# A Swin block on one core: FC2 in float16 with its scale in PSUM, tokens turned in spans of 112, and the step loop written out

## The chip, the core and the metric

The kernel runs on one core of a Trainium2 chip. A core has TensorE (PE; its weight loads are shown apart as PEld), VectorE (DVE), ScalarE (ACT), GpSimd (POOL) and SyncE (SP, which here issues all DMAs). Each has its own instruction stream, and they wait for each other through semaphores. Products are written to PSUM, which the kernel uses as eight banks of 512 float32 columns; GpSimd works on SBUF alone here. The metric is the device time of one execution in microseconds, the median of several runs.

## The reference

A window-attention block on x of 32 x 96 x 56 x 56 (float32): layer norm over the 96 channels, a shift by 3, windows of 7 x 7 = 49 tokens, 12 heads of 8 channels, a mask for the shifted borders, a projection, then an MLP of 96 -> 192 -> 96 with an exact GELU, and two residuals.

```python
f = _ln(x.transpose(0, 2, 3, 1), g1, b1); f = jnp.roll(f, (-SS, -SS), axis=(1, 2))
qkv = _window_partition(f) @ w_qkv + b_qkv                      # -> q, k, v
attn = softmax(q @ k.T * scale + mask); out = (attn @ v) @ w_proj + b_proj
f = residual + roll(_window_reverse(out), (SS, SS))
m = _ln(f, g2, b2)
m = jax.nn.gelu(m @ w_fc1 + b_fc1, approximate=False) @ w_fc2 + b_fc2
return f + m
```

## The kernel before, in words

**Tiling.** The image is cut into bands of seven rows: eight windows, 392 tokens (`TOK`). There are 32 x 8 = 256 bands. A tile has channels on partitions and a band's 392 tokens in the free dimension, or tokens on partitions. All products that need precision are made of float16 halves: weights and tokens are split into a high and a low part, and three products (high x high, high x low, low x high) are summed in PSUM, with the weights times `GAIN` = 64.

**Pipeline.** Work is a pipeline over steps. In step t each engine runs a fixed list of stages, each for another band: `LOAD` for band t+9, `TURN` for t+6, `BACK` for t+5, `QK` for t+4, `VALUES` and `SCORE` for t+2, `PROB` for t, `WEIGH` for t-1, and in pairs `HIDDEN` (FC1 and GELU), `RESULT` (FC2) and `STORE` for bands around t-5 to t-7. Odd and even steps have different lists: FC1 and GELU of two bands stand in the odd step (`expand`, `expand_rest`, `gelu`), FC2 of two bands at the end of PE's even step (`contract`). The order in each engine is written by hand; each engine takes its instructions strictly in that order. What a stage must wait for is counted from the band's number.

**The loop.** `steps` (L186) writes out the steps -9 to 8, then a `Fori` loop of seven rounds of 32 steps, then the rest. In the loop the counts that semaphores are compared with are computed from a register.

**The token turns (L516, L541).** PE's `turn` transposes the normalised-to-be tokens from channels on partitions to tokens on partitions: x of band t+6 (tile `xw`) and, for the second layer norm, the residual sum of eight bands earlier (tile `f`). Each is four transposes of 98 tokens into one bank each (D and D+1). ACT (even steps) or DVE (odd steps) copies them to `tok`; DVE makes statistics per group of 98 tokens (`bn_stats`, `bn_aggr`, eight groups); POOL's `normalise` makes `xn` (subtract the mean, a power of -1/2, multiply); PE's `back` transposes the eight groups back into banks B and B+1, ACT's `back_high` (L703) writes the float16 high part `xfh`, DVE's `back_low` (L844) the low part `xfl`.

**FC2 (L620).** `contract` waits for `gelu_done` and the free banks D, D+1, and multiplies in float32, which the trace records as two passes per product:

```python
for s in range(2):
    dst = psum[0:C, D + n, s * PART:(s + 1) * PART]
    nc.tensor.matmul(dst, w2[:, 0, :], hid[:, b.c % 2, s, :], start=True, stop=False)
    last = nc.tensor.matmul(dst, w2[:, 1 + s, :], hid[:, b.c % 2, 2, :], start=False, stop=True)
```

POOL's `add_bias` (L370) adds the FC2 bias to `f` beforehand, and DVE's `result` (L864) adds `f` and the bank into `yr`, which SP stores.

**What stands around FC2.** In the even step PE's list ends with `out_transposes` (L591), `back` (L553), `max_transpose` (L580), `queries_keys` (L420), `project` (L601), `contract` 0 and 1 (L632, L633). The odd step's list begins with `shifted(t, 0)` (L494), which waits for `stack_in`, `max_in` and, at L489, for `n_low` of the even step's `back`; then `values` (L455) and `scores(t, 0)` (L476), which waits for `qk_low`. ACT in the even step: `queries_keys_high` (nat, L714), then `back_high` (xfh, L706), then the odd step's `exps` (L694). DVE: `back_low` (L847), `queries_keys_low` (L854), `result`. POOL in each step: `normalise`, `order_x` (copies a loaded band into window order), `add_bias`.

## Time and profile before

| | |
|---|---|
| median of 3 runs | 2933.02 us (2930.35 to 2939.53) |
| the profiled execution | 2936.45 us, its span 2934.7 us |
| mean granted TensorE clock | 0.994 |
| PE busy | 2835.0 us, 97% of the span |
| DVE busy | 2404.5 us, 82% |
| ACT busy | 2000.5 us, 68% |
| POOL busy | 1758.0 us, 60% |
| DMA | 359.65 MB, mean 123 GB/s |

Busy is the union of an engine's instruction times. Matmuls overlap each other, so the distance from one start to the next tells what one costs in a stream, not its own length. The chain is followed back from the last instruction: at each step to whatever ended the wait, so its shares tell which engine's work made up the span. "Issue" is time in the chain in which the profile shows nothing that was waited for.

### The profile page before, as it was taken

How to read it: one execution, taken by the hardware profiler on the slowest of the kernel's cores; microseconds unless marked ns; L12 is line 12 of the kernel's file. 1: busy time of each engine (PE TensorE's matmuls, PEld its weight loads, DVE VectorE, ACT ScalarE, POOL GpSimd, SP SyncE). 2: the span in 40 equal slices, each digit the busy share in tenths (PEclk: the TensorE clock that was granted, in tenths of full speed). 3: DMA queues.
4: the chain of work that ended last, by engine and by line, in shares of the span. 5: the costliest groups of instructions: out<-in, count | busy, mean ns of one | idle time of the engine just before them, and what ended most of it. 6: DMA issues, size and time to landing. Idle time of an engine off the chain costs nothing.

```text
span 2934.7 us, 141485 instructions
## 1 busy us (share of the span) xinstructions
PE 2835.0 (97%) x54820; PEld 2387.2 (81%) x54820; DVE 2404.5 (82%) x7142; ACT 2000.5 (68%) x3208; POOL 1758.0 (60%) x2088
## 2 busy tenths in 40 slices
PE   4999999999999999999999999999999999999997
PEld 2788888888878888888888888878888788888886
DVE  6888887888878888788888888878888788888885
ACT  2676776777767777667766776767777677677674
POOL 3566566566656666565665666656666556656655
PEclk9999999999999999999999999999999999999999
DMA  3444454445444554444444444445445444444441
GB/s 83 121 130 127 127 130 120 129 122 131 130 118 120 129 131 121 123 126 130 122 131 122 128 128 130 124 118 130 130 119 133 117 129 128 127 126 129 125 117 43
DMA packets 414934, 359.65 MB, mean 123 GB/s; under 512 B 63646, under 2 KB 414176, under 8 KB 414204
## 3 DMA queue, kind: packets, MB, share of 16 engines
q1 hardware_dynamic: 414220, 350.04, 45.8%
q8 instruction: 459, 7.52, 1.1%
q14 instruction: 255, 2.09, 0.2%
HBM read 193.29 MB, written 154.14 MB: 118 GB/s over the span
## 4 chain that ended last, share of the span: by engine, by line
PE 90%; ACT 5%; issue 2%; DVE 2%; POOL 0%; SPq 0%; DMA 0%; DVEq 0%; ACTq 0%; POOLq 0%
PE psum L512 19%; PE psum L494 11%; PE psum L420 8%; PE psum L476 8%; PE psum L538 7%; PE psum L553 6%; PE psum L601 6%; PE psum L632 6%; PE psum L633 6%; PE psum L430 5%; ACT probs L694 4%; PE psum L591 3%; PE psum L438 3%; PE psum L455 2%; PE psum L580 1%
## 5 line engine op out<-in xcount | busy, mean ns | idle before, releaser
L694 ACT ACTIVATE probs<-psum 113x784 f32<-113x784 f32 x768 | 632.3, 823 | 642.8 <-PE psum L494 639.7
L812 DVE TENSOR_REDUCE nmax<-psum 113x16 f32<-113x784 f32 x768 | 745.0, 970 | 148.0 <-PE psum L476 147.6
L383 POOL TENSOR_SCALAR ve<-mv 98x8 f32<-98x8 f32 (+1 forms) x264 | 63.6, 241 | 1082.3 <-DVE mv L841 1082.3
L512 PE MATMUL psum<-vbd,probs 128*49 128x18 f32 x24576 | 641.4, 198 | 4.1 <-issue 3.8
L512 PEld LDWEIGHTS psum<-vbd,probs 128*49 128x49 f32 x24576 | 631.5, 126 | 6.9 <-issue 6.2
L494 PE MATMUL psum<-qbd,kst 128*49 128x196 f16 x6144 | 401.6, 251 | 36.0 <-DVE xfl L847 25.8
L390 POOL TENSOR_TENSOR rs<-ve,half 98x8 f32<-98x8 f32 (+1 forms) x264 | 435.0, 1648 | 0.0
L395 POOL TENSOR_TENSOR xn<-xn,rs 98x768 f32<-98x768 f32 (+1 forms) x264 | 382.8, 1450 | 74.5 <-POOL rs L390 74.2
L836 DVE BATCH_NORM_STATS2 st<-tok 98x6 f32<-98x96 f32 x2080 | 359.4, 245 | 71.8 <-ACT tok L701 56.8
L476 PE MATMUL psum<-kbd,qst 128*49 128x196 f16 x6144 | 398.7, 250 | 5.7 <-DVE nmax L812 3.2
L386 POOL TENSOR_TENSOR xn<-tok,mv 98x768 f32<-98x768 f32 (+1 forms) x264 | 384.5, 1456 | 0.6 <-POOL ve L383 0.6
L847 DVE TENSOR_TENSOR xfl<-psum,xfh 96x784 f16<-96x784 f32 (+1 forms) x264 | 252.8, 958 | 105.5 <-ACT xfh L706 104.1
L476 PEld LDWEIGHTS psum<-kbd,qst 128*49 128x49 f16 x6144 | 264.1, 104 | 82.2 <-issue 77.5
L376 POOL TENSOR_SCALAR f<-f,vec 96x392 f32<-96x392 f32 x256 | 325.3, 1271 | 0.0
L494 PEld LDWEIGHTS psum<-qbd,kst 128*49 128x49 f16 x6144 | 236.8, 104 | 99.5 <-issue 60.3
L714 ACT ACTIVATE nat<-psum 96x784 f16<-96x784 f32 x256 | 209.8, 819 | 124.9 <-PE psum L420 124.9
L688 ACT ACTIVATE vbd<-psum 49x384 f32<-49x384 f32 x512 | 260.9, 510 | 7.6 <-PE psum L455 1.3
L632 PE MATMUL psum<-hid,w 128*96 128x196 f32 x1024 | 254.5, 330 | 1.1 <-ACT hid L736 1.1
L633 PE MATMUL psum<-hid,w 128*96 128x196 f32 x1024 | 254.3, 330 | 0.0
L553 PE MATMUL psum<-ident,xn 98*96 98x98 f32 x2080 | 223.4, 250 | 24.9 <-POOL xn L395 23.8
L854 DVE SCALAR_TENSOR_TENSOR nat<-psum,nat 96x784 f16<-96x784 f32 x256 | 245.7, 960 | 0.0
L706 ACT ACTIVATE xfh<-psum 96x784 f16<-96x784 f32 (+1 forms) x264 | 212.3, 804 | 25.1 <-PE psum L553 25.0
(90 smaller groups left out, 5638.2 us busy)
## 6 DMA issues: line engine op xcount, KB each, us to landing
stack_pages<-nat SPq DMA_DIRECT2D x256, 294.0 KB, 3.1
kst<-stack_pages SPq DMA_DIRECT2D x256, 220.5 KB
qbd<-stack_pages SPq DMA_DIRECT2D x1024, 55.1 KB
stack_pages<-nat SPq DMA_DIRECT2D x256, 147.0 KB, 2.1
xr<-in_x_dram SPq DMA_DIRECT2D x224, 147.0 KB, 2.5
out_dram<-yr SPq DMA_DIRECT2D x224, 147.0 KB, 2.1
qst<-stack_pages SPq DMA_DIRECT2D x256, 73.5 KB
kbd<-stack_pages SPq DMA_DIRECT2D x1024, 18.4 KB
```

The lines of the kernel that those rows point to most:

```text
L386: nc.gpsimd.tensor_tensor(xn[:, n, 0:groups, :], tok[:, n, :, :, :].rearrange("t k p c -> t (k p) c")[:, 0:groups, :], mv[:, n, 0:groups, ...
L390: nc.gpsimd.tensor_tensor(rs[:, n, 0:groups], ve[:, n, 0:groups], half[0:PT, 0:groups], ALU.pow).then_inc(root_done, 1)
L395: nc.gpsimd.tensor_tensor(xn[:, n, 0:groups, :], xn[:, n, 0:groups, :], rs[:, n, 0:groups].rearrange("t (g a) -> t g a", a=1).to_broadcast ...
L476: last = nc.tensor.matmul(psum[W1 * w:W1 * w + L, A + p // 2, p % 2 * CH:(p % 2 + 1) * CH], qst[:, masked_slot(b), u, toks], kbd[:, b.c % ...
L494: last = nc.tensor.matmul(psum[W1 * w:W1 * w + L, B + p // 2, p % 2 * CH:(p % 2 + 1) * CH], kst[:, masked_slot(b), u, toks], qbd[:, b.c % ...
L512: last = nc.tensor.matmul(dst[:, :, h, :], probs[:, b.c % 2, h // 4, p, h % 4 * L:(h % 4 + 1) * L], vbd[:, b.c % 4, p * NH + h, :, :], sta ...
L553: last = nc.tensor.transpose(psum[0:C, B + kind, p * PT:(p + 1) * PT], xn[:, b.c % 2, kind * PAIRS + p, :], ident[0:PT, 0:PT])
L632: nc.tensor.matmul(dst, w2[:, 0, :], hid[:, b.c % 2, s, :], start=True, stop=False)
L633: last = nc.tensor.matmul(dst, w2[:, 1 + s, :], hid[:, b.c % 2, 2, :], start=False, stop=True)
L694: nc.scalar.activation(probs[0:PR, b.c % 2, u, :, :].rearrange("j (g q) k -> j g (q k)", g=2), psum[0:PR, B:B + 2, 0:2 * CH], ACT.Exp).the ...
L812: nc.vector.tensor_reduce(dst, psum[0:PR, A:A + 2, 0:2 * CH].rearrange("i g (q h j) -> i g q h j", q=2, j=L), axis=AX.X, op=ALU.max, negat ...
L836: last = nc.vector.bn_stats(st[:, n, g, :], tok[:, n, g // PAIRS, g % PAIRS, :])
```

## The change

1. All steps are written out: `steps` has no `Fori` loop any more, and all counts are constants.
2. FC2 is made of float16 products. At the start DVE's `split_w2` multiplies `w2` by `GAIN` and splits it into `w2h` and `w2l`. POOL's `split_hidden` copies the GELU's result to float16 (`hidh`) and subtracts to get `hidl`, for two bands ahead of the even step's other POOL stages; `add_bias` is gone. `contract` waits for `hid_low` and makes twelve products of 196 columns per band. `gelu` waits in addition for the split of two bands earlier.
3. ACT's `scaled`, at the end of the even step, applies 1/`GAIN` and the bias to the FC2 bank in place (Identity, PSUM to PSUM); DVE's `result` waits for it in place of the product and the bias.
4. x and the residual sum lie side by side in one tile `xf`, so that the 784 tokens of both are turned in seven spans of 112 (`SPAN`) in place of eight of 98. The spans by token lie 128 columns apart in banks D and D+1; the ones turned back lie without a gap over banks B and B+1 from column 64 (`LEFT`), and `shifted`/`exps` use the same layout. In odd steps `back` repeats its last span behind the others.

The diff, cut to its core:

```diff
+SPAN = 112
+GROUPS = 2 * TOK // SPAN
+LEFT = 512 - 4 * SPAN
         def steps(engine, step):
-            for t in range(-LOAD, FIRST):
-                step(Band(None, t))
-            with engine.Fori(0, rounds) as i:
-                for t in range(TURNS * BANDS):
-                    step(Band(i, FIRST + t))
-            for t in range(FIRST + TURNS * BANDS * rounds, NB - STORE[1]):
+            for t in range(-LOAD, NB - STORE[1]):
                 step(Band(None, t))
+        def spans(b):
+            return GROUPS if kinds(b) == 2 else -(-TOK // SPAN)
+        def by_token_bank():
+            return psum[:, D:D + 2, :].rearrange("p b (g r) -> p (b g) r", g=4)
+        def wide_bank():
+            return psum[:, B:B + 2, :].rearrange("p b r -> p (b r)")
+        def by_channel(b):
+            return wide_bank()[0:C, LEFT:LEFT + kinds(b) * TOK]
...
-            def add_bias(b):
-                pool.wait_ge(t_made, b.step(AFTER).count(1, 1))
-                nc.gpsimd.tensor_scalar(f[:, b.c % 8, :], f[:, b.c % 8, :], vec[:, BF:BF + 1], None, ALU.add).then_inc(f_biased, 1)
+            def split_hidden(b):
+                n = b.c % 2
+                pool.wait_ge(gelu_done, b.count(1, 1))
+                wait(pool, fc2_made, b.count(1, -1))
+                alone(pool)
+                nc.gpsimd.tensor_copy(hidh[:, n, :, :], hid[:, n, :, :]).then_inc(hid_high, 1)
+                pool.wait_ge(hid_high, b.count(1, 1))
+                alone(pool)
+                nc.gpsimd.tensor_tensor(hidl[:, n, :, :], hid[:, n, :, :], hidh[:, n, :, :], ALU.subtract).then_inc(hid_low, 1)
...
             def step(t):                                   # POOL
                 filling = t.i is None and t.c < 0
+                if not odd(t):
+                    for offset in RESULT:
+                        if has(t.step(offset)):
+                            split_hidden(t.step(offset))
...
-                if has(t.step(BIAS)):
-                    add_bias(t.step(BIAS))
...
                 alone(pe)                                  # turn
-                for kind, (one, src, n) in enumerate(((b, xw, 8), (before, f, 8))):
-                    if has(one):
-                        for p in range(PAIRS):
-                            last = nc.tensor.transpose(psum[0:PT, D + kind, p * C:(p + 1) * C], src[:, one.c % n, p * PT:(p + 1) * PT], ident[0:C, 0:C])
+                both = xf[:, b.c % 8, :, :].rearrange("c k t -> c (k t)")
+                for g in range(spans(b)):
+                    last = nc.tensor.transpose(by_token_bank()[0:SPAN, g, 0:C], both[:, g * SPAN:(g + 1) * SPAN], ident[0:C, 0:C])
...
-                for kind in range(kinds(b)):               # back
-                    for p in range(PAIRS):
-                        last = nc.tensor.transpose(psum[0:C, B + kind, p * PT:(p + 1) * PT], xn[:, b.c % 2, kind * PAIRS + p, :], ident[0:PT, 0:PT])
+                order = list(range(spans(b)))
+                for at, g in enumerate(order + order[-1:] if odd(t) and has(t.step(HIDDEN[0])) else order):
+                    last = nc.tensor.transpose(wide_bank()[0:C, LEFT + at * SPAN:LEFT + (at + 1) * SPAN], xn[:, b.c % 2, g, :], ident[0:SPAN, 0:SPAN])
...
+                pe.wait_ge(hid_low, b.count(1, 1))         # contract
                 if n == 0:
-                    pe.wait_ge(gelu_done, b.count(1, 2))
...
                 for s in range(2):
                     dst = psum[0:C, D + n, s * PART:(s + 1) * PART]
-                    nc.tensor.matmul(dst, w2[:, 0, :], hid[:, b.c % 2, s, :], start=True, stop=False)
-                    last = nc.tensor.matmul(dst, w2[:, 1 + s, :], hid[:, b.c % 2, 2, :], start=False, stop=True)
+                    for k, (weights, part) in enumerate(((0, s), (1 + s, 2))):
+                        for m, (w, h) in enumerate(((w2h, hidh), (w2h, hidl), (w2l, hidh))):
+                            last = nc.tensor.matmul(dst, w[:, weights, :], h[:, b.c % 2, part, :], start=k + m == 0, stop=k == 1 and m == 2)
...
+                wait(act, hid_low, b.count(1, -1))         # gelu
+            def scaled(t, n):
+                b = t.step(RESULT[n])
+                act.wait_ge(fc2_made, b.count(1, 1))
+                nc.scalar.activation(psum[0:C, D + n, 0:TOK], psum[0:C, D + n, 0:TOK], ACT.Identity, bias=vec[:, BF:BF + 1], scale=1 / GAIN).then_inc(y_scaled, 1)
...
+                    run(RESULT[0], scaled, 0)              # ACT, end of the even step
+                    run(RESULT[1], scaled, 1)
...
+            def split_w2():
+                nc.vector.tensor_scalar(w2[:, :, :], w2[:, :, :], GAIN, None, ALU.mult).then_inc(w2_wide, 1)
+                dve.wait_ge(w2_wide, 1)
+                nc.vector.tensor_copy(w2h[:, :, :], w2[:, :, :]).then_inc(w2_split, 1)
+                dve.wait_ge(w2_split, 1)
+                nc.vector.tensor_tensor(w2l[:, :, :], w2[:, :, :], w2h[:, :, :], ALU.subtract).then_inc(w2_wide, 1)
...
-                dve.wait_ge(fc2_made, b.count(1, 1))       # result
-                dve.wait_ge(f_biased, b.count(1, 1))
+                dve.wait_ge(y_scaled, b.count(1, 1))
```

## Rows read from the trace of the kernel before

**Rows 1.** The page's chain that ended last, by engine.

```profile
PE 90%; ACT 5%; issue 2%; DVE 2%; POOL 0%; SPq 0%; DMA 0%; DVEq 0%; ACTq 0%; POOLq 0%
```

**Rows 2.** Busy by stretch: start:end, length, then busy per engine (instructions), PEclk, DMA, GB/s.

```profile
...
848.52:878.15 29.63, 25.71 (x430) 22.03 (x429) 19.18 (x56) 16.51 (x26) 13.51 (x16) 0.86 0.41 104
...
sum 161.77, PE 139.99 PEld 118.86 DVE 111.41 ACT 94.85 POOL 81.09; mean PE 23.33 PEld 19.81 DVE 18.57 ACT 15.81 POOL 13.52
```

**Rows 3.** Busy by stretch, the same columns: a steady pair of steps.

```profile
1477.80:1499.76 21.96, 21.87 (x431) 18.49 (x430) 18.46 (x56) 15.64 (x26) 13.52 (x16) 1.00 0.49 127
```

**Rows 4.** Chain in order of time (start, us, what), through one loop return.

```profile
506.27 3.99 issue
...
511.96 0.12 issue
512.09 0.85 PE psum L494 x8
```

**Rows 5.** Timeline of PE, an even step's end: start, us, engine, line, shapes, count.

```profile
1510.22 0.49 PE L538 MATMUL psum<-ident,f 96*98 96x96 f32 x4
1510.55 0.55 PE L591 MATMUL psum<-ident,on 113*96 113x113 f32 x4
1510.94 0.84 PE L553 MATMUL psum<-ident,xn 98*96 98x98 f32 x8
1511.61 0.26 PE L580 MATMUL psum<-ident,nmax 113*48 113x113 f32 x1
1511.71 0.33 PE L420 MATMUL psum<-xfh,wh 128*96 128x392 f16 x1
...
1512.71 0.82 PE L601 MATMUL psum<-oT,wp 128*96 128x392 f32 x2
1513.37 0.49 PE L632 MATMUL psum<-hid,w 128*96 128x196 f32 x2
1513.70 0.49 PE L633 MATMUL psum<-hid,w 128*96 128x196 f32 x2
...
1516.11 0.53 PE L494 MATMUL psum<-qbd,kst 128*49 128x196 f16 x8
...
1516.99 0.51 PE L476 MATMUL psum<-kbd,qst 128*49 128x196 f16 x8
```

**Rows 6.** Timelines of ACT and DVE in the same step, after FC2's start.

```profile
1512.91 0.82 ACT L714 ACTIVATE nat<-psum 96x784 f16<-96x784 f32 x1 [0.67 <-PE psum L420]
1513.63 0.81 ACT L706 ACTIVATE xfh<-psum 96x784 f16<-96x784 f32 x1
...
1514.47 0.97 DVE L847 TENSOR_TENSOR xfl<-psum,xfh 96x784 f16<-96x784 f32 x1 [0.20 <-ACT xfh L706]
1515.36 0.96 DVE L854 SCALAR_TENSOR_TENSOR nat<-psum,nat 96x784 f16<-96x784 f32 x1
```

**Rows 7.** Groups by line: what, count, busy us, mean ns, idle before; weight loads.

```profile
L553 PEld LDWEIGHTS psum<-ident,xn 98*96 98x96 f32 x2080 | 184.5, 127 | 45.5 <-POOL xn L395 25.2 <-issue 9.5
```

**Rows 8.** Groups by line and shape, ACT.

```profile
L736 ACT ACT_TABLE_LOAD x126 | 161.7, 1283 | 2.3
L706 ACT ACTIVATE xfh<-psum 96x392 f16<-96x392 f32 x8 | 3.9, 487 | 17.8 <-PE psum L553 17.8
```

**Rows 9.** Groups by line and shape, POOL.

```profile
L386 POOL TENSOR_TENSOR xn<-tok,mv 98x768 f32<-98x768 f32 x256 | 377.9, 1476 | 0.6 <-POOL ve L383 0.6
L376 POOL TENSOR_SCALAR f<-f,vec 96x392 f32<-96x392 f32 x256 | 325.3, 1271 | 0.0
L364 POOL COPY xw<-xr 96x343 f32<-96x343 f32 x256 | 126.3, 493 | 7.4 <-DMA xr<-in_x_dram 7.1 <-POOL vbd L354 0.3
L367 POOL COPY xw<-xr 96x28 f32<-96x28 f32 x256 | 53.0, 207 | 0.0
...
L386 POOL TENSOR_TENSOR xn<-tok,mv 98x384 f32<-98x384 f32 x8 | 6.6, 827 | 0.0
```

**Rows 10.** Timeline of POOL, the odd step before FC2.

```profile
1509.47 1.27 POOL L376 TENSOR_SCALAR f<-f,vec 96x392 f32<-96x392 f32 x1
```

## What the change does to the time: the prediction

> **What bounds the kernel now.** I read the shares of the chain of waits first: TensorE holds 90% of it, no other engine over 5% [rows 1]. So this is a kernel in which TensorE's own instruction stream is the time, and an edit counts by what it does to that stream. Next the busy table by stretches. The steps repeat in pairs (odd, even), and a stretch from one odd step's first expand product to the next takes 21.96 us with 21.87 us of PE busy [rows 3]; steady pairs differ from 21.94 by hundredths. Six stretches out of 127 are far longer, up to 29.63 us, 161.77 us together, with the same instruction count [rows 2]. They lie 16 pairs, so 32 steps, apart: they are the returns of the `Fori` loop. The chain through one of them [rows 4] shows 3.99 us of "issue" in which VectorE runs nothing, then VectorE catching up, and PE's L494 released 0.12 us after xfl ends. Last the order of time around the FC2 products in a steady pair [rows 5, 6], because that is where a shorter PE stream can meet a wait that it covers today.
>
> **Steps written out.** The six stretches hold 161.77 - 6 x 21.94 = 30.1 us over their steady length [rows 2, 3]: the idle fetch, the catching up of the slower engines, and matmuls at the lower of the two clock levels after the pause (PEclk 0.86 in the worst stretch, so part of it at 1.2 GHz). Without a loop there is no return, and all 30.1 us go. Can straight code cost something in exchange? Each pass of the body is 32 steps of straight code already, 16 pairs long, and between returns no such gap appears; so I take nothing. Bounds: none of the gain, or all of it and the 9 us that the small bumps of the other pairs add up to.
>
> **FC2 in float16 on PE.** Before, a pair has 16 recorded float32 passes of 196 columns, from 1513.37 to the start of L494 at 1516.11: 2.74 us, of which 16 x 0.1655 = 2.65 us is stream and 0.09 us the turnaround to L494 (L633 starts 0.33 us after L632's two) [rows 5]. After it has 24 float16 products of 196 columns (2 bands x 2 halves x 2 weight blocks x 3). No row shows this form. The nearest is L420: six float16 products of 392 columns in 1.00 us, 0.167 us each; half of it is 0.0835, I take 0.084 us. That supposes that the weight loads stay hidden. Bounds: 0.0815 us below, and 0.127 us above, the busy time of one load [rows 7], if a load were never hidden. I take the lower end, because in the same row's products (L553) a load of 127 ns busy goes with one product each 0.084 us [rows 5, 7]. So 24 x 0.084 = 2.02 us and 0.63 us less per pair; at the upper bound it would be 3.05 us, 0.40 us more than now.
>
> The Trainium skill ("TensorE: Matmul & The Clock Gate", Back-to-back issue gap) speaks against the change here: in a stream of load and matmul pairs it gives about 81 ns per 128-column product, where columns alone would be 56, and for a load P/1.2, 80 ns for 96 columns. An estimate by that page's 25 ns surcharge is 24 x 0.109 = 2.62 us, which would leave 0.03 us of the 0.63. The trace disagrees with it for this stream: L553 and L420 show a load before each product and no such surcharge.
>
> **Spans of 112 rows on PE.** Turning in goes from 8 to 7 transposes per step, each 0.083 us (four in 0.33 us, L538 to L591): 0.165 us less per pair. The moving side is the 96-wide identity, as before; the wider stationary side (112 for 98) is hidden like the rest. Turning back goes from 8 at 0.084 us (0.67 us for eight, L553 to L580) to 7 in even and 8 in odd steps (the last one is repeated) with 112 moving columns. L591 with 113 columns takes 0.0975 us each [rows 5], so 15 x 0.097 - 16 x 0.084 = 0.11 us more. PE's stream so far: -0.63 - 0.165 + 0.11 = -0.685 us per pair.
>
> **The wait that becomes visible.** After FC2, PE's next instruction is L494 of the odd step, and it waits for n_low, which VectorE's xfl gives. Everything of PE is queued behind it. ScalarE starts nat at 1512.91, then xfh, which ends 1514.44; xfl runs from 1514.47 to 1515.44 [rows 6]. Add the release of 0.12 us [rows 4]: L494 can't start before 1515.56. It now starts at 1516.11; with 0.63 us less in front it would be 1515.48. So 0.08 us come back as a wait. In some pairs nat starts about 0.1 us later; I take 0.10 us on average. The next wait in line, scores on qk_low, has the same margin: L854 ends at 1516.32, plus 0.12 is 1516.44, while L476 (1516.99 now) would come at 1516.44 with L494 at 1515.56. It adds nothing or hundredths. Bounds for both together: 0 and 0.3 us.
>
> **ScalarE.** Two Identity activations of 96x392 per pair, 0.487 us each by the row of that size [rows 8]. The first can start when the first band's FC2 is done (1513.37 + 1.01 + 0.16, so 1514.54, just after xfh) and the second at about 1515.55; it ends 1516.04, and the odd step's first exp can't start before L494's eight products are in, about 1516.1. They lie in an idle stretch (1514.44 to L494's end) and cost nothing. Without that cover each would push the exps by 0.49 us. If Identity forced a table change, two loads of 1.283 us [rows 8] would come per pair; the trace has two loads per pair only, at Exp and at Gelu, though Copy activations stand between. The Trainium skill ("ScalarE: Activation LUTs", Table sets: the hidden batching unit) lists identity among the fillers of every set; no row here shows it.
>
> **VectorE.** bn_stats and bn_aggr lose one group each per step, the copy of tokens gets 96 columns shorter; `result` now waits for the scaled bank (1516.04) and starts after L854 anyway (1516.32). VectorE is no slower; I count none of it. `split_w2` runs once, about 1 us in the filling: +1 us.
>
> **GpSimd.** It loses the bias (1.271 us per band) and 96 columns in each of normalise's two wide operations (slope between 384 and 768 columns 1.69 ns, so 0.32 us per step) [rows 9]. It gains per band a copy to float16 and a subtraction of 128x588. No row shows float16 on this engine. By the float32 rows: copy 0.493 us at 343 and 0.207 at 28 columns gives 0.72 us at 588; tensor_tensor 1.476 - 180 x 0.00169 = 1.17 us. Both bands with two gaps of 0.27 us: 4.3 us. Bound above: the slowest pace per column of any row, L376's 1.271 us for 392, so 1.91 us for each, 8.2 us with the gaps. I take the float32 rows, which are the same two operations. The two splits stand in the even step ahead of normalise, so right behind the odd step's order_x. Its end is 1509.47 in the pair shown [rows 10]; 1509.15 after. The splits then end near 1511.3 and 1513.45. PE needs the first before 1513.3 and the second before 1514.4 (one band's FC2 later). 2 and 0.95 us to spare, so nothing is paid. Normalise of the even step, behind them, starts today at about 1514 by VectorE's statistics, so it isn't pushed.
>
> **Sum.** The profiled execution took 2936.45 us (span 2934.7). 124 pairs run at the steady rate; each loses 0.685 - 0.10 = 0.585 us: 72.5 us. 2936.5 - 30.1 - 72.5 + 1 = 2834.9 us. The median of the runs shown (2933.02) lies 3.4 us below the profiled one: 2832 us. A steady pair should measure 21.36 us.
>
> **The rivals.**
> - Slower: GpSimd is late with hidl. Place: contract of the second band, all of PE behind it. Price: at L376's pace the second split ends at 1509.15 + 8.2 = 1517.35, 2.95 us late; a pair takes 21.94 - 0.685 + 2.95 = 24.2 us, and the kernel 2936.5 - 30.1 + 124 x 2.27 - 3.4 = 3184 us. It costs from copy plus subtraction over 2.36 us per band (I have 1.89), and the kernel is slower than before once PE waits over 0.685 + 0.24 = 0.93 us, which is 2.83 us per band. For it: no float16 row, and one float32 operation here at nearly twice the pace per column. Against: that one has a per-partition scalar operand, and the two new ones haven't. Chance 0.10.
> - The same in small, or the waits on n_low, qk_low and s_maxed adding up to 0.3 us or more: 2865 to 2920 us. For it: three margins here are under 0.2 us. Chance 0.17.
> - Loads not wholly hidden. Halfway between the bounds of 2.02 and 3.05 us nearly all of the FC2 gain is gone: about -0.1 us per pair, 2936.5 - 30.1 - 12 - 3.4 = 2891 us. The page's surcharge named above gives about the same, 2892 us. Chance 0.05.
> - Identity changes the table: the first exp of the odd step ends near 1518.3 and L494's second group waits about 0.5 us: +62, so 2894 us. Chance 0.04.
> - Straight code doesn't run without pauses, or the returns weren't the cause: 30 us stay, 2862 us. Chance 0.04.
> - The forecast, 2805 to 2860 us: 0.60.
>
> The lower end of the range is no new wait and no bumps (2936.5 - 30.1 - 86 - 9 - 3.4 = 2808) with a little room; the upper takes in the loads and the table. GpSimd's heavy case is left out: 2803 to 2896 us. 0.3% is about 9 us. Slower holds GpSimd's case (0.10) and 0.01 more; the same 0.03 is a moderate delay of GpSimd that eats just the gain; faster 0.86.
>
> **What would show it.** Steady pairs at 21.3 to 21.4 us between L430's groups, and no pair over 23 us; the FC2 products at 0.084 us from start to start; a wait "PE L494 <- DVE xfl" of about 0.1 us in every odd step; two Identity activations just under 0.5 us and still two table loads per pair; on GpSimd 0.7 and 1.2 us for the split, and no "PE <- POOL hidl" wait. Wrong would be: a PE wait on hidl, float16 products spaced 0.1 us or more, three table loads or more per pair, or gaps of several us that stay.

## The result, and the profile after

The changed kernel takes 2865.91 us (median of 4 executions, 2864.05 to 2867.5); the kernel before, in the same set, 2935.6 us. The ratio is 0.9754 (95% interval 0.9731 to 0.9777): 2.5% faster. Forecast were 2832 us and a range of 2803 to 2896. Direction and mechanism hold, but a third of the gain is missing: 69.0 us less span (2934.7 to 2865.7) where the sum had 101.6. The time lies above the 2805 to 2860 us that the forecast held most likely (0.60), at the lower edge of the rival of small waits (2865 to 2920 us, chance 0.17).

The page of the changed kernel, its busy line and its chain by engine (before: [rows 1]):

```profile
PE 2765.1 (96%) x55491; PEld 2312.9 (81%) x55491; DVE 2349.2 (82%) x6634; ACT 2136.4 (75%) x3464; POOL 1810.7 (63%) x2344
...
PE 91%; ACT 4%; issue 2%; DVE 2%; POOL 1%; SPq 0%; DMA 0%; POOLq 0%; DVEq 0%
```

TensorE lost 70 us of busy time and still holds 91% of the chain; ScalarE gained 136 us and GpSimd 53 us of busy time, and their shares of the chain went from 5 to 4% and from 0 to 1%. A steady pair of steps, busy by stretch as in [rows 3], from one odd step's first expand product to the next:

```profile
1420.31:1441.86 21.55, 21.33 (x435) 17.91 (x435) 18.02 (x52) 16.69 (x28) 13.93 (x18) 1.00 0.49 129
```

21.55 us, where the median before was 21.94 (the pair of [rows 3] took 21.96) and 21.36 was forecast. The chain of waits of the changed kernel through the end of an even step (start, us, what) shows where the missing part is:

```profile
1411.76 0.66 PE psum L617 x2
1412.42 2.02 PE psum L652 x24
1414.45 0.14 issue
1414.59 0.53 PE psum L511 x8
...
1419.65 0.72 PE psum L554 x7
1420.37 0.60 PE psum L447 x3
```

The 24 FC2 products (L652) take exactly the 2.02 us forecast. Behind them is a hole: 0.14 us of "issue", and with it the first L511 (L494 before) starts 0.39 us after the last L652 product, where one without a wait follows after 0.084 us, and L511 itself after 0.177 in run 1 below. What PE waits for there, ACT and DVE in the changed kernel (two timelines; before: [rows 6]):

```profile
1411.80 0.82 ACT L733 ACTIVATE nat<-psum 96x784 f16<-96x784 f32 x1 [0.75 <-PE psum L437]
1412.52 0.81 ACT L725 ACTIVATE xfh<-psum 96x784 f16<-96x784 f32 x1
1413.47 0.56 ACT L763 ACTIVATE psum<-psum,vec 96x392 f32<-96x392 f32 x1
1414.48 0.55 ACT L763 ACTIVATE psum<-psum,vec 96x392 f32<-96x392 f32 x1 [0.46 <-PE psum L652]
```

```profile
1413.36 0.97 DVE L884 TENSOR_TENSOR xfl<-psum,xfh 96x784 f16<-96x784 f32 x1 [0.28 <-ACT xfh L725]
1414.26 0.96 DVE L891 SCALAR_TENSOR_TENSOR nat<-psum,nat 96x784 f16<-96x784 f32 x1
```

xfl ends at 1414.33 and L511 starts at 1414.59: the release takes 0.26 us (median of all pairs 0.257), not 0.12. GpSimd's split of the second band in the same step, and the groups by line and shape of the new work:

```profile
1409.78 0.67 POOL L388 CAST hidh<-hid 128x588 f16<-128x588 f32 x1
1410.63 1.30 POOL L391 TENSOR_TENSOR hidl<-hid,hidh 128x588 f16<-128x588 f32 x1 [0.18 <-POOL hidh L388]
```

```profile
L391 POOL TENSOR_TENSOR hidl<-hid,hidh 128x588 f16<-128x588 f32 x256 | 334.1, 1305 | 46.2 <-POOL hidh L388 46.2
...
L388 POOL CAST hidh<-hid 128x588 f16<-128x588 f32 x256 | 172.9, 676 | 5.3 <-ACT hid L756 5.3
L756 ACT ACT_TABLE_LOAD x126 | 161.7, 1283 | 2.2
L713 ACT ACT_TABLE_LOAD x125 | 160.4, 1283 | 2.2
L763 ACT ACTIVATE psum<-psum,vec 96x392 f32<-96x392 f32 x256 | 141.9, 554 | 88.0 <-PE psum L652 71.2
L652 PEld LDWEIGHTS psum<-hidl,w2h 128*96 128x96 f16 x1024 | 127.7, 125 | 25.8 <-issue 25.8
```

The second hidl is ready at 1411.93, while the second band's products start at 1413.27, 1.34 us later: GpSimd is not late. There are still two table loads per pair, so Identity forces none. The FC2 weight loads (125 ns busy) go at 84 ns each beside the products.

The whole difference, taken between the starts of the odd steps' first expand products:

| part of the span | forecast, us | measured, us |
|---|---|---|
| steady pair: 124 x -0.585, against 123 x -0.389 | -72.5 | -47.9 |
| the six loop returns | -30.1 | -30.1 |
| what the other pairs take over a steady one (mostly small pauses), 9.0 to 12.1 | 0 | +3.0 |
| filling, 118.8 to 119.5 | +1 | +0.7 |
| tail after the last of these pairs, 78.1 to 83.4 | 0 | +5.3 |
| sum | -101.6 | -69.0 |

In the tail no step's other work covers GpSimd any more. The chain of the changed kernel there (start, us, what):

```profile
2830.15 0.63 POOL hidh L388
...
2830.98 1.27 POOL hidl L391
2832.25 0.63 POOL hidh L388
...
2833.05 1.31 POOL hidl L391
2834.35 0.04 issue
2834.40 0.62 PE psum L652 x5
```

Two splits, 4.2 us, stand open on the chain, where the kernel before went from GELU to FC2 at once. Run 8 below, which has no split, has a tail of 78.4 us.

### The profile page after: what moved, and what is told of

It reads as the page before. It is cut to its first block, busy times and chain, and to the rows that moved or that the text cites. A ratio compares the mean times of both kernels' runs of the same rounds, so it can differ in the third digit from the quotient of the medians.

```text
span 2865.7 us, 137800 instructions
## 1 busy us (share of the span) xinstructions
PE 2765.1 (96%) x55491; PEld 2312.9 (81%) x55491; DVE 2349.2 (82%) x6634; ACT 2136.4 (75%) x3464; POOL 1810.7 (63%) x2344
## 3 DMA queue, kind: packets, MB, share of 16 engines
q8 instruction: 447, 7.32, 1.1%
## 4 chain that ended last, share of the span: by engine, by line
PE 91%; ACT 4%; issue 2%; DVE 2%; POOL 1%; SPq 0%; DMA 0%; POOLq 0%; DVEq 0%
PE psum L529 19%; PE psum L511 11%; PE psum L652 9%; PE psum L437 9%; PE psum L493 8%; PE psum L569 7%; PE psum L554 6%; PE psum L617 6%; PE psum L447 6%; ACT probs L713 4%; PE psum L607 3%; PE psum L455 3%; PE psum L472 2%; PE psum L596 1%; DVE nmax L849 0%
## 5 line engine op out<-in xcount | busy, mean ns | idle before, releaser
L529 PE MATMUL psum<-vbd,probs 128*49 128x18 f32 x24576 | 642.4, 197 | 7.6 <-issue 7.0
L398 POOL TENSOR_SCALAR ve<-mv 112x7 f32<-112x7 f32 (+1 forms) x264 | 65.9, 250 | 915.0 <-PE psum L569 672.8
L529 PEld LDWEIGHTS psum<-vbd,probs 128*49 128x49 f32 x24576 | 632.2, 126 | 10.7 <-issue 10.5
L511 PE MATMUL psum<-qbd,kst 128*49 128x196 f16 x6144 | 404.7, 250 | 34.4 <-DVE xfl L884 5.7
L493 PE MATMUL psum<-kbd,qst 128*49 128x196 f16 x6144 | 404.5, 250 | 5.3 <-DVE nmax L849 3.4
L405 POOL TENSOR_TENSOR rs<-ve,half 112x7 f32<-112x7 f32 (+1 forms) x264 | 394.7, 1495 | 0.0
L410 POOL TENSOR_TENSOR xn<-xn,rs 112x672 f32<-112x672 f32 (+1 forms) x264 | 342.6, 1298 | 73.9 <-POOL rs L405 73.9
L873 DVE BATCH_NORM_STATS2 st<-tok 112x6 f32<-112x96 f32 x1824 | 318.1, 246 | 59.0 <-ACT tok L720 45.0
L391 POOL TENSOR_TENSOR hidl<-hid,hidh 128x588 f16<-128x588 f32 x256 | 334.1, 1305 | 46.2 <-POOL hidh L388 46.2
L401 POOL TENSOR_TENSOR xn<-tok,mv 112x672 f32<-112x672 f32 (+1 forms) x264 | 343.4, 1301 | 0.5 <-POOL ve L398 0.5
L493 PEld LDWEIGHTS psum<-kbd,qst 128*49 128x49 f16 x6144 | 270.1, 104 | 82.4 <-issue 77.3
L511 PEld LDWEIGHTS psum<-qbd,kst 128*49 128x49 f16 x6144 | 243.6, 103 | 87.7 <-issue 48.2
L652 PE MATMUL psum<-hidh,w2h 128*96 128x196 f16 x1024 | 255.9, 250 | 4.2 <-POOL hidl L391 4.2
L569 PE MATMUL psum<-ident,xn 112*96 112x112 f32 x1951 | 236.3, 263 | 23.1 <-POOL xn L410 22.1
L652 PE MATMUL psum<-hidh,w2l 128*96 128x196 f16 x1024 | 254.8, 249 | 0.0
L652 PE MATMUL psum<-hidl,w2h 128*96 128x196 f16 x1024 | 254.5, 249 | 0.0
```

The source lines that it names most:

```text
L391: nc.gpsimd.tensor_tensor(hidl[:, n, :, :], hid[:, n, :, :], hidh[:, n, :, :], ALU.subtract).then_inc(hid_low, 1)
L401: nc.gpsimd.tensor_tensor(xn[:, n, 0:groups, :], tok[:, n, 0:groups, :], mv[:, n, 0:groups, 0:1].to_broadcast(wide_by_token), ALU.subtract ...
L405: nc.gpsimd.tensor_tensor(rs[:, n, 0:groups], ve[:, n, 0:groups], half[0:SPAN, 0:groups], ALU.pow).then_inc(root_done, 1)
L410: nc.gpsimd.tensor_tensor(xn[:, n, 0:groups, :], xn[:, n, 0:groups, :], rs[:, n, 0:groups].rearrange("t (g a) -> t g a", a=1).to_broadcast ...
L493: last = nc.tensor.matmul(psum[W1 * w:W1 * w + L, A + p // 2, p % 2 * CH:(p % 2 + 1) * CH], qst[:, masked_slot(b), u, toks], kbd[:, b.c % ...
L511: last = nc.tensor.matmul(wide_bank()[W1 * w:W1 * w + L, LEFT + p // 2 * 4 * SPAN + p % 2 * CH:LEFT + p // 2 * 4 * SPAN + (p % 2 + 1) * CH ...
```

## The experiments

Each was timed against the kernel before on the same chip. The kernel before varied between chips (medians 2937.8, 2942.2 and 2953.5 us), so I compare the ratios, the spans and the pairs.

**1. The order on ScalarE (e_order).** Shortens the chain to n_low and leaves PE's list as it is. In the changed kernel:

```diff
-                    run(QK, queries_keys_high)
                     if turns(t.step(BACK)):
                         back_high(t)
+                    run(QK, queries_keys_high)
                     run(RESULT[0], scaled, 0)
```

> The changed kernel with one edit: in even steps ScalarE makes xfh (back_high) ahead of nat (queries_keys_high), as it does in odd steps. Theory (the gain that is missing went into a wait of PE's first instruction of the odd step on n_low, 0.21 us per pair): xfh ends about 0.75 us sooner, xfl begins when the residual is done (about 0.28 us sooner than now), n_low then comes before PE is free, and a steady pair falls from 21.55 to about 21.34 us: some 26 us less than the changed kernel, about 2840 us. Rival (that gap is PE's own turnaround, or the pair is set elsewhere, by exps or GpSimd): the pair stays at 21.55 us and the time at 2866 us, or it grows since nat and then qk_low come later.

Measured: 2831.14 us, ratio 0.9592 (0.9557 to 0.9627), span 2829.3, steady pair 21.35 us. Its chain at the same place, with no "issue" between the products:

```profile
1413.12 2.03 PE psum L652 x24
1415.15 0.46 PE psum L511 x8
```

L511 starts 0.177 us after the last L652 product (0.392 in the changed kernel). The visible wait was worth 0.20 us per pair, 24.6 us in all, near the 26 of the theory; 7.0 us more, which it did not have, went with fewer small pauses (the other pairs' excess fell from 12.1 to 5.0 us), 4.4 in the filling and 0.4 in the tail, 36.4 us of span together. This is the fastest version that I ran: 4.1% under the kernel before, 1.3% under the changed one (2829.3 against 2865.7 us of span). The wait on n_low is the cause of the mis-sized pair.

**2. The order of PE's waits (e_waitfirst).** Same waits, same work, only the wait on n_low is written first:

```diff
+                    pe.wait_ge(n_low, t.step(BACK - 1).count(1, 1))
                     pe.wait_ge(stack_in[b.c % 4], b.used(4, STACK_IN))
                     pe.wait_ge(max_in[b.c % 2], b.used(2, 16))
-                    pe.wait_ge(n_low, t.step(BACK - 1).count(1, 1))
```

> The changed kernel with the n_low wait of shifted written ahead of the waits on stack_in and max_in, so that the last one to come isn't followed by two more wait instructions. In the changed kernel 0.257 us pass from the end of xfl to the first product behind it, in the kernel before 0.133 us at a loop return. Theory (the rest of that release is the sequencer working off the other waits behind n_low): 0.05 to 0.12 us less per pair, 21.43 to 21.50 us, 6 to 15 us less than the changed kernel. Rival (the release takes this long whatever the order): 21.55 us and 2866 us.

Measured: 2846.89 us, 0.9646 (0.9611 to 0.9681), span 2845.4, pair 21.42. The pair and the time fell slightly more than the theory's 21.43 to 21.50 us and 6 to 15 us. From xfl's end to L511 it is now 0.054 us (median of 125 places) in place of 0.257. DVE and PE's weight loads (PEld) at one such place of this run:

```profile
1401.68 0.97 DVE L884 TENSOR_TENSOR xfl<-psum,xfh 96x784 f16<-96x784 f32 x1 [0.28 <-ACT xfh L725]
```

```profile
1402.70 0.30 PEld L511 LDWEIGHTS psum<-qbd,kst 128*49 128x49 f16 x8
```

The same load in the changed kernel, where xfl ended at 1414.33:

```profile
1414.56 0.33 PEld L511 LDWEIGHTS psum<-qbd,kst 128*49 128x49 f16 x8 [0.32 <-issue]
```

So 0.20 us of the release was not the semaphore's way from VectorE to PE. The trace's wait instructions of PE show where it was, and their order is not the written one: the wait that is written first is carried by the weight load itself and so comes last. In the changed kernel n_low, written third, is a wait instruction of its own that comes first and ends 0.09 us after xfl; a second wait instruction, for two other semaphores, ends at 0.20, the load with a fourth wait starts at 0.23 and the product at 0.257. In this run the two wait instructions start at 1401.10 and 1401.21, well before xfl's end at 1402.65, and n_low is on the load, which starts 0.05 us after xfl. Of these 0.20 us, 0.08 came back at once as the next wait in line (scores on qk_low: from the first L511 to the first L493 0.93 us, 0.85 before), which leaves the 0.13 us of the pair.

**3. One product fewer (e_eight).**

```diff
-                        for m, (w, h) in enumerate(((w2h, hidh), (w2h, hidl), (w2l, hidh))):
+                        for m, (w, h) in enumerate(((w2h, hidh), (w2h, hidl))):
```

> Leaves work out: FC2 without its third product (w2l x hidh), so 16 float16 products per pair where the changed kernel has 24, 0.67 us of PE less. Theory (n_low ends the wait behind FC2, so PE's stream there no longer counts): the gap before L511 grows by 0.67 us and the pair stays at 21.55 us, the time within 5 us of 2866. Rival (PE's stream sets the pair there): 20.9 us per pair, 2783 us.

Measured: 2912.12 us, 0.986 (0.9817 to 0.9903), span 2908.6: 43 us longer than the changed kernel with eight products fewer in every pair. Its chain through two such places:

```profile
1411.63 0.82 ACT nat L733
1412.45 0.72 ACT xfh L725
1413.17 0.02 issue
1413.20 0.98 DVE xfl L884
1414.18 0.25 issue
1414.43 0.53 PE psum L511 x8
...
1439.12 0.07 PE psum L529 x3
1439.19 0.40 issue
1439.59 1.14 PE psum L529 x42
```

The first part answers the question: the shorter FC2 is off the chain, ACT and DVE are on it, and the shortest pairs stay at 21.55 us (34 of the 123 take under 21.6). The second part is what neither theory had: 0.40 us in which PE stands still between two equal products with nothing to wait for. The waits of PE in this kernel (in total, times, longest) against those of the changed kernel:

```profile
PE psum L529 <- issue: 27.4, 45, 1.1
...
PE psum L511 <- issue: 8.8, 10, 1.2
PE psum L493 <- issue: 8.2, 8, 2.2
```

```profile
PE psum L529 <- issue: 7.0, 15, 0.9
```

Counted between products of the same line, there are 60 pauses of 38.6 us in all, and 22 of 7.9 us in the changed kernel. That is 30.7 of the 43 us; the rest, among it some twenty pairs of 21.64 us, was not taken apart. So the time alone doesn't settle the question; run 9 does.

**4. The loop put back (e_loop).**

```diff
-            for t in range(-LOAD, NB - STORE[1]):
+            for t in range(-LOAD, FIRST):
                 step(Band(None, t))
+            with engine.Fori(0, rounds) as i:
+                for t in range(TURNS * BANDS):
+                    step(Band(i, FIRST + t))
+            for t in range(FIRST + TURNS * BANDS * rounds, NB - STORE[1]):
+                step(Band(None, t))
```

> The changed kernel with the step loop put back (seven rounds of 32 steps), all else as it is. Theory: six returns again, 5 us each over a steady pair, 30 us together; and if a wait folded into a register instruction is what made the release 0.133 us long in the loop, the steady pair inside the loop is 21.43 us, 14 us back over the loop's pairs: 2880 to 2885 us. Rival (the release has nothing to do with it): 30 us more, 2896 us. Rival (straight code has a price of its own in the small pauses of PE, 12 us where the loop had 9): 3 us less than either.

Measured: 2920.82 us, 0.99 (0.9864 to 0.9936), span 2912.1: slower than the theory and both rivals said. The six returns lie 33.0 us over the pairs around them, and the pair behind each is another 1.4 us long, 8.6 us. The steady pairs did not fall to 21.43 us; most alternate between 21.55 and 21.68 us. The chain of this kernel in one of the longer ones:

```profile
1435.79 0.04 ACTq L210
1435.82 0.04 issue
1435.86 0.02 ACTq L210
1435.88 0.04 issue
1435.92 0.05 ACT nat L740
```

ScalarE works off two waits (L210) before nat, which starts 0.13 us later; with the wait on n_low visible, each hundredth of that chain is on PE's path. In the kernel before it was covered: there the first L494 starts 0.671 us after xfl's end in one pair and 0.538 in the next, and the pair stays at 21.94. So with the rest of the change in place the loop costs 46 us of span, against 18.7 us in the kernel before (run 6); by the ratios of the medians it is 43 and 21 us. Writing the steps out is worth more together with the new FC2 than alone.

**5. The changed kernel on another chip (e_after_again).** No edit.

> The changed kernel itself, unedited, as the base of the other three on one chip. Every theory: 21.55 us per steady pair. The kernel before took 2935.6 us on one chip and 2953.5 us on another; if the 18 us between them are the loop's returns, this one takes 2866 us here too; if they are the chip's, it takes about 18 us more.

Measured: 2866.8 us, 0.974 (0.9711 to 0.9769), span 2865.6, pair 21.55. The place and size of the loss belong to the program, not to the chip.

**6. Steps written out alone (e_before_out).** In the kernel before:

```diff
-            with engine.Fori(0, rounds) as i:
-                for t in range(TURNS * BANDS):
-                    step(Band(i, FIRST + t))
...
+            for t in range(-LOAD, NB - STORE[1]):
+                step(Band(None, t))
```

> The kernel before with its steps written out and nothing else changed. Theory (the returns are worth 30 us in the profiled run and nothing else depends on them): 21.94 us per steady pair, no pair over 24 us, 30 us less than the kernel before, or more where its returns cost more on this chip. Rival (written-out steps also save or cost in the steady pairs, by the waits that were folded into register instructions): the steady pair moves by 0.05 us or more.

Measured: 2920.64 us, 0.9927 (0.9904 to 0.9951), span 2916.0, pair 21.94. The 30.1 us of the returns are gone and the pair is untouched; but 7.6 us came as small pauses (excess over the steady pair 16.6 us for 9.0), 2.0 in the filling and 1.8 in the tail: 18.7 us of span gained.

**7. Spans of 98 (e_span98).** In the changed kernel:

```diff
-SPAN = 112
+SPAN = 98
...
-            nc.vector.memset(xf[:, :, 1, 0:4 * SPAN - TOK], 0.0)
```

> The changed kernel with spans of 98 tokens in place of 112 (eight spans; back repeats its last one in odd steps, nine there). Theory (the odd step's turn is covered by the wait on exp_done before expand, so only the even step's counts): even turn +0.083, odd turn +0.01, back -0.03 us: 21.61 us per pair, some 8 us more than the changed kernel. Rival (turn counts in both steps, as I predicted): 21.69 us, 17 us more. Rival (the longer work of VectorE and GpSimd makes the split late): over 21.75 us and PE waits on hidl.

Measured: 2874.12 us, 0.9765 (0.9737 to 0.9794), span 2872.2, pair 21.60. With this layout, spans of 112 are worth 0.05 us a pair against spans of 98, some 6 us. They are no part of the 69 us, though: here the odd step turns nine spans back (the last one twice), where the kernel before turned eight. Against the kernel before, the terms below give +0.015 us a pair for the whole of this edit, and run 8 has 0.04 us at most.

**8. FC2 in float32 again (e_fc2_f32).** No split on GpSimd, and `contract` waits for `gelu_done` again; Identity stays, with its place and size:

```diff
-                        for m, (w, h) in enumerate(((w2h, hidh), (w2h, hidl), (w2l, hidh))):
...
+                        last = nc.tensor.matmul(dst, w2[:, weights, :], hid[:, b.c % 2, part, :], start=k == 0, stop=k == 1)
```

> The changed kernel with the FC2 products back in float32 on the unsplit GELU result, without the split on GpSimd (the Identity activation stays, its factor is now wrong by 64, so FC2's result is left out of the right scale). Theory (float16 saves 0.63 us of PE, of which the wait on n_low takes 0.21 us back): the pair is 21.96 us, 51 us more than the changed kernel, and there is no wait before L511's first product. Rival (no such wait, the whole 0.63 us counts): 22.18 us, 78 us more.

Measured: 2924.68 us, 0.9935 (0.9912 to 0.9958), span 2922.7, pair 21.98. So the float16 FC2 is worth 0.43 us a pair (0.63 less the 0.21 of the wait), 53 us, and Identity costs next to nothing: with it and the spans of 112 the pair is where the kernel before was, within 0.04 us. The first L507 (L494 before) starts 0.67 us after xfl's end, so there is no wait.

**9. The third product short (e_eight_short).** As run 3, but with the same number of instructions:

```diff
+                            cols = 16 if m == 2 else PART
-                            last = nc.tensor.matmul(dst, w[:, weights, :], h[:, b.c % 2, part, :], start=k + m == 0, stop=k == 1 and m == 2)
+                            last = nc.tensor.matmul(dst[:, 0:cols], w[:, weights, :], h[:, b.c % 2, part, 0:cols], start=k + m == 0, stop=k == 1 and m == 2)
```

> Leaves work out: the third FC2 product (w2l x hidh) covers 16 of its 196 columns, so PE has the same number of instructions as the changed kernel and 0.4 to 0.5 us less work per pair. The run without that product was 46 us slower than the changed kernel, and its pauses of PE came at one place modulo 256 PE instructions. Theory (n_low hides PE's shorter stream, and the added time was pauses of the instruction fetch, which depend on how many instructions are used up in how little time): the gap before L511 grows, the pair stays at 21.55 us, and what is over it is small pauses, more than the changed kernel's 8 us since the stream that consumes a block is no shorter in all but denser in one place: 2866 to 2880 us. Rival (dense FC2 or the shorter stretch disturbs something else in the steady pair): 2900 us or more with the same instruction count.

Measured: 2865.87 us, 0.9752 (0.9723 to 0.9781), span 2863.2, pair 21.55, 23 pauses of 8.0 us, no more than in the changed kernel, where the theory had more. The last FC2 product stands 0.67 us before L511 in place of 0.39. Both halves are settled: a shorter FC2 gives nothing while n_low is late, and run 3's loss came from taking instructions out of PE's stream, not from taking out time. The number alone does not do it either: run 8 has as few instructions on PE as run 3 (112398) and 31 pauses of 10.7 us.

**10. One turn fewer in odd steps (e_turn6).**

```diff
-                for g in range(spans(b)):
+                for g in range(spans(b) - (1 if odd(t) else 0)):
```

> Leaves work out: the odd step's turn transposes one span less, 0.083 us less PE work per pair. Theory (the first expand product behind it waits for the last exp of the step, exp_done, and starts 0.145 us after that exp's end whatever PE does before): 21.55 us per pair, the changed kernel's time within 3 us. Rival (PE's stream counts there, as my sum had it): 21.47 us, 10 us less.

Measured: 2864.91 us, 0.9748 (0.972 to 0.9777), span 2864.7, pair 21.55. Six turns or seven in the odd step: no difference. The expand product behind them waits for the last exp. That is visible in the changed kernel, on ACT and on PE:

```profile
1419.34 0.82 ACT L713 ACTIVATE probs<-psum 113x784 f32<-113x784 f32 x1 [1.08 <-PE psum L511]
```

```profile
1420.31 0.33 PE L447 MATMUL psum<-xfh,w1h 128*128 128x392 f16 x1
```

The exp ends at 1420.16 and the product starts 0.15 us later; the gap between the two was 0.15 us in the kernel before as well.

**11. Both orders (e_order_swap).** Run 1, and in PE's even step:

```diff
                     scores(t, 0)
-                    weighted(t, 0)
                     shifted(t, 0)
+                    weighted(t, 0)
                     values(t)
```

> The changed kernel with ScalarE's even step in the order xfh, nat, and PE's even step with shifted 0 ahead of weighted 0. In the changed kernel PE waits in every even step at shifted 1 for the first exp, which starts only when shifted 0 is done, 0.4 us after ScalarE's table load; about 0.23 us between L493's last product and L511's next. Theory (with shifted 0 first, that exp starts right behind the table load and ends before PE comes to shifted 1): 21.35 less 0.2 us per pair, 21.12 to 21.2 us, 2805 to 2815 us. Rival (the wait moves on to the second exp or to n_low of the odd step's back): 21.35 us, 2831 us or slower.

Measured: 2856.08 us, 0.9715 (0.9678 to 0.9752), span 2852.2: slower than run 1, and the expectation missed. The commonest pair does come down, to 21.28 us (21.12 to 21.2 expected), but 19 of the 123 lie between 21.9 and 22.5. PE's waits in it:

```profile
PE psum L529 <- issue: 19.4, 34, 1.1
```

54 pauses, 24.9 us, where run 1 has 10 with 2.0 us, with the same number of instructions on PE (114446). It isn't only the number, then, but what stands where in the stream.

**12. GpSimd made to be late (e_pool_thrice).** Two more casts per band, into a tile that nobody reads:

```diff
+                nc.gpsimd.tensor_copy(hidx[:, 0, :, :], hid[:, n, :, :])
+                nc.gpsimd.tensor_copy(hidx[:, 1, :, :], hid[:, n, :, :])
                 nc.gpsimd.tensor_copy(hidh[:, n, :, :], hid[:, n, :, :]).then_inc(hid_high, 1)
```

> The changed kernel with two more copies of the GELU's result per band on GpSimd, of no use, 1.35 us per band and 2.7 us per pair. In the changed kernel the second hidl ends about 1.2 us before PE needs it, and the wait on n_low behind FC2 covers another 0.2 us. Theory (the split is hidden by that margin, and past it every us counts in full): PE waits for hidl, 21.55 + 2.7 - 1.4 = 22.85 us per pair, 3025 to 3030 us. Rival (normalise behind the split, or the next step's order, moves too and the delay adds up): 23.5 us or more. Rival (GpSimd has more room than I read): under 22 us.

Measured: 2979.4 us, 1.0142 (1.0113 to 1.0172), span 2977.7, pair 22.42. The wait that the slower rival spoke of, on PE:

```profile
PE psum L655 <- POOL hidl L394: 124.2, 131, 4.1
```

2.5 us more on GpSimd (four casts, 0.62 us from start to start) cost 0.87 us a pair, so about 1.6 us of room was there: the 1.34 us between hidl and the second band's products and the 0.2 us of the wait on n_low, not the 0.95 of the prediction. The pair lies between the theory's 22.85 us and the under 22 us of the rival with more room. The slower rival of the prediction was a real mechanism; its price per column was wrong, not its place.

## Why the prediction was right in kind and 34 us off

**Steps written out: the term holds, the "nothing in exchange" doesn't.** The returns gave back 30.1 us, as forecast. Run 6 shows straight code costing 11.4 us on the kernel before; with the whole change the small pauses grew by 3.0 us. The sentence that failed is "between returns no such gap appears; so I take nothing": the small ones were in the trace, 9 us of them, and I set them down as a bound and not as a term.

**FC2 in float16: right.** 24 products in 2.02 us, 0.084 us each, loads hidden (125 ns busy each, one per product). By an estimate with the 25 ns surcharge worked out from the Trainium skill ("TensorE: Matmul & The Clock Gate", Back-to-back issue gap) it would have been 2.62 us; the trace disagrees.

**Spans of 112: half right.** Turning back costs 0.11 us more (0.81 to 0.90 us odd, 0.68 to 0.70 even), as forecast. Turning in gives 0.08 us in each step, but in the odd step 0.07 us of it is lost: the expand's first three products take 0.60 us of the chain for 0.53, since they wait for the exps. So the whole edit, forecast at -0.055 us, comes to +0.015 us a pair and gained nothing. The sum counted instructions of PE in a place where ScalarE sets the time. I had looked for a late wait only behind FC2; run 10 shows this second one.

**The wait that becomes visible: the step that failed.** Named rightly, with the right chain (nat, xfh, xfl, release), and put at 0.10 us. It is 0.21: from the end of the last queries-and-keys product to L511 the kernel before takes 3.24 us; less 0.63 would be 2.61, and 2.83 are measured. The size came from the release of 0.12 us at a loop return [rows 4]. There the trace has one register instruction of PE's sequencer (0.04 us) between xfl's end and the weight load. In the steady pairs of the changed kernel it has two wait instructions one after the other, as told at run 2: the one on n_low ends 0.09 us after xfl, the one on two more semaphores 0.20 after it, and the load starts at 0.23; 0.257 us to the product. The kernel before covers that: its L494 starts 0.671 us after xfl's end (0.538 in every second pair), so 0.63 us less leaves 0.04, and 0.257 are needed. The row was the nearest in time and not the nearest in kind. Run 1, which takes the wait away, lands at 21.35 us, the pair that I had forecast with 0.10 us of wait and the whole of both turns.

So per pair: FC2 -0.63, turning in -0.165 and 0.07 of it back, turning back +0.11, the wait +0.21, which is -0.40; measured -0.39. Over 123 pairs the two mis-sized terms make 0.18 x 123 = 22 us.

**ScalarE and VectorE: right.** Identity takes 0.554 us for the 0.487 taken, costs no table load and is covered (run 8). **GpSimd: right, with more room than I gave it** (0.676 and 1.305 us for 0.72 and 1.17). What I missed is the tail, where two splits stand on the chain for 4.2 of the 5.3 us; in run 8, without the splits (and with FC2 in float32), the tail is 78.4 us, as before.

**Left out of the sum:** tail 5.3, pauses 3.0, and one pair less than counted. With the 22 us these make up the 33 us between -101.6 and -69.0, to some 2 us.

**Luck and slips.** The range held because its upper end was set by rivals that did not happen (loads not hidden, a table change). The rival of small waits named the right place, but with 0.3 us or more of waiting; 0.21 us and the terms left at nothing reached its time. Two sums were slightly off: 124 x 0.685 is 84.9, not 86, in the lower end, and halfway between the bounds of the loads leaves a gain of about 0.17 us per pair with the spans, not 0.1, so 2882 us and not 2891.

## What to carry to other kernels

When a shortened stream meets a wait at the bound engine, look for the producers' order first: two activations exchanged on ScalarE gave half as much again as the whole change, with no work saved. Work out a release only from a place with the same waits in the same order. Look in the trace for the order in which the waits are worked off: here the one written first came last, on the weight load, and that is the place for the wait that is satisfied last. And before counting an instruction that is taken from the bound engine's stream, ask of every step (not only of the one that changed) whether the instruction behind it already waits for another engine.

## What the runs showed of the hardware

**Pauses at fixed places of the instruction stream.** TensorE stands still between equal products with nothing to wait for, mostly for 0.1 to 1.2 us (1.44 at most, in run 11). I counted PE's instructions, loads and products together: in every written-out kernel these pauses come at the same count modulo 256 (194 or 195); in the kernel before, with its loop, at 176 to 194, drifting from round to round, and in run 4 at several counts that change from round to round. Packets of the instruction queue q8 are 16384 bytes and mostly take 0.9 to 1.4 us. There are 447 of them in the changed kernel (7.32 MB) for PE's 114446 instructions, so 256 instructions in each, 64 bytes per instruction. The pauses come mostly within L529, where PE does about 45 short products a microsecond, each with its load:

| kernel | pauses | us |
|---|---|---|
| before | 14 | 4.6 |
| run 6, before written out | 28 | 8.1 |
| changed | 22 | 7.9 |
| run 1 | 10 | 2.0 |
| run 8, FC2 in float32 | 31 | 10.7 |
| run 9, third product short | 23 | 8.0 |
| run 3, third product left out | 60 | 38.6 |
| run 11 | 54 | 24.9 |

The Trainium skill ("Runtime: NRT & Kernel Launch", Instruction fetch mechanics) says that instructions are fetched in 16 KiB blocks of 256 and that crossing a block boundary is mostly hidden. The places agree with the blocks; "mostly hidden" holds for run 1 and not for runs 3 and 11. The times agree too: in run 3 each of the 60 pauses ends 1.2 to 1.7 us after the latest of these packets has landed, while at the 374 boundaries without a pause PE comes to that place a median of 4.0 us after it (run 11: 54 pauses at 1.2 to 1.6 us, the others 3.8). So a pause stands where PE arrives early for its packet. That the late fetch is the cause is still inferred from places and times and not shown by a run of its own, and I can't say beforehand which arrangement of instructions is a bad one. Two small edits to this kernel changed its pauses by 20 to 30 us (run 3 against the changed kernel, run 11 against run 1), so the pauses have to be counted apart before the time is read.

**The order of waits costs, even when the others are satisfied.** A product started 0.257 us after the semaphore that came last when the wait on it was worked off first, with one more wait instruction and the load's own wait behind it, and 0.054 us after it when that wait was the last one, on the weight load itself (run 2).
